# Sparse experts of a graph-network layer: row gathers four slots ahead, finished rows in buffers of their own, slot 0 always expert 0

## What is computed

```python
x = x + sparse(_layernorm(x))
# sparse:
gate_logits = x @ gate_w.T + gate_b + expert_bias        # 1250 x 8
top_idx = argmax(gate_logits, axis=-1)                   # one expert per row
for e in range(8):
    h = relu(x @ w1[e] + b1[e])                          # 1024 -> 512
    y = h @ w2[e] + b2[e]                                # 512 -> 1024
    out = out + (top_idx == e) * y
```

## Time and profile before

| what | us |
|---|---|
| median of 3 runs (2924.33 to 2933.4) | 2929.55 |
| the profiled execution | 2930.76 |
| its span | 2929.0 |
| TensorE busy | 2697.2 (92%) |
| VectorE busy | 1433.2 (49%) |
| ScalarE busy | 763.5 (26%) |
| GpSimd busy | 751.0 (26%) |

### The profile page before, as it was taken

One profiled execution on the slowest core, in us unless ns is written; L12 is line 12 of the kernel. 1 busy time (PEld: TensorE's weight loads), 2 busy tenths in 40 slices (PEclk: granted clock), 3 DMA queues, 4 the chain that ended last, 5 costly groups with the idle time before them and its releaser, 6 DMA issues.

```text
span 2929.0 us, 32304 instructions
## 1 busy us (share of the span) xinstructions
PE 2697.2 (92%) x11128; PEld 2018.5 (69%) x11128; DVE 1433.2 (49%) x2411; ACT 763.5 (26%) x1241; POOL 751.0 (26%) x738
## 2 busy tenths in 40 slices
PE   5998998889999979999999999999999997958887
PEld 3553333478888767888888888887777676836775
DVE  8886775555455481001001001007888887846543
ACT  2002221233233232112112112114444443114321
POOL 1326771000000004555400000104555450003333
PEclk9999999799999988999999999999999998978998
DMA  4016773023333231222222222226777784437763
GB/s 136 1 64 194 210 211 86 1 87 115 115 115 115 86 143 58 99 78 90 93 75 107 76 79 104 93 75 201 236 233 262 256 253 174 137 138 252 261 245 106
DMA packets 168160, 399.86 MB, mean 137 GB/s; under 512 B 25152, under 2 KB 25920, under 8 KB 168072
## 3 DMA queue, kind: packets, MB, share of 16 engines
q0 software_dynamic: 56384, 168.89, 18.7%
q1 hardware_dynamic: 84472, 180.00, 17.7%
q10 hardware_dynamic: 27216, 49.86, 4.6%
HBM read 327.74 MB, written 75.25 MB: 138 GB/s over the span
## 4 chain that ended last, share of the span: by engine, by line
PE 76%; DMA 9%; DVE 8%; issue 3%; ACT 2%; POOL 1%; DVEq 0%; ACTq 0%; POOLq 0%; SPq 0%
PE pair L899 10%; PE pair L901 10%; PE pair L900 10%; PE pair L795 5%; DMA out<-tok_x,tok_put 3%; DMA tok_x<-x_rows,tok_list 3%; PE pair L737 3%; PE pair L810 2%; PE pair L777 2%; PE pair L922 2%; PE pair L945 2%; PE pair L943 2%; PE pair L944 2%; PE pair L925 2%; PE pair L865 2%
## 5 line engine op out<-in xcount | busy, mean ns | idle before, releaser
L1560 DVE TENSOR_TENSOR wl<-raw,wh 128x512 fp32r<-128x512 f32 x328 | 205.4, 686 | 802.0 <-ACT wh L1062 801.9
L899 PE MATMUL pair<-wh,xh 128*128 128x512 f32 x1280 | 499.0, 390 | 1.7 <-DVE xl L1311 1.7
L901 PE MATMUL pair<-wl,xh 128*128 128x512 f32 x1280 | 498.7, 390 | 0.0
L900 PE MATMUL pair<-wh,xl 128*128 128x512 f32 x1280 | 498.6, 390 | 0.0
L658 POOL DMA_INDIRECT rows_y<-y_rows,l_row x184 | 222.3, 1208 | 303.6 <-PE pair L925 156.7
L1062 ACT ACTIVATE OS<-pair 128x512 f32<-128x512 f32 x170 | 101.5, 597 | 746.9 <-PE pair L901 693.4
L899 PEld LDWEIGHTS pair<-wh,xh 128*128 128x128 f32 x1280 | 240.8, 188 | 52.2 <-issue 2.1
L900 PEld LDWEIGHTS pair<-wh,xl 128*128 128x128 f32 x1280 | 240.8, 188 | 50.2
L901 PEld LDWEIGHTS pair<-wl,xh 128*128 128x128 f32 x1280 | 240.7, 188 | 50.0
L1062 ACT ACTIVATE high_y<-rows_y,l_inv 128x1024 fp32r<-128x1024 f32 x154 | 176.6, 1151 | 252.1 <-DMA rows_y<-y_rows,l_row 239.2
L1062 ACT ACTIVATE wh<-raw 128x512 fp32r<-128x512 f32 x328 | 194.0, 627 | 182.3 <-PE pair L867 140.5
(11 more groups left out here) (275 smaller groups left out, 4610.4 us busy)
## 6 DMA issues: line engine op xcount, KB each, us to landing
y_rows<-OS ACTq DMA_DIRECT2D x160, 256.0 KB, 2.0
raw<-in_L_gnn_weight SPq DMA_DIRECT2D x16, 2048.0 KB, 8.9
raw<-in_L_ffn_w SPq DMA_DIRECT2D x12, 2048.0 KB, 8.9
raw<-in_L_ffn_w SPq DMA_DIRECT2D x24, 1024.0 KB, 6.2
tok_raw<-in_L_ffn_w SPq DMA_DIRECT2D x7, 2048.0 KB, 10.9
tok_raw<-in_L_ffn_w SPq DMA_DIRECT2D x14, 1024.0 KB, 14.1
U<-in_L_ffn_b SPq DMA_DIRECT2D x18, 512.0 KB, 4.4
x_rows<-X SPq DMA_DIRECT2D x1, 5120.0 KB, 15.3
```

The lines of the kernel that those rows point to most:

```text
L899: mm(o, xh[:, k, cols], wh[:, k, :], start=(k == 0), stop=False)
L900: mm(o, xl[:, k, cols], wh[:, k, :], start=False, stop=False)
L901: last = mm(o, xh[:, k, cols], wl[:, k, :], start=False, stop=(k == KD - 1))
L1560: v.tensor_tensor(wl[:, k, :], raw[:, k, :], wh[:, k, :].bitcast(F32), ALU.subtract).then_inc(wl_ready, 1)
```

## The change

- Weights of expert 0 for slot 0 are loaded before the routing is known: w1, b1 and b2 as soon as the last rows of the stage before are mixed, w2 when the layer norm has read them and they are stored. ScalarE makes the high parts right behind the route matmuls, VectorE the low parts of w1 in two places of the routing (`first_w1_low`); the low parts of w2 stay where they were. `sort` gets `least=1`: expert 0 has at least one slot.
- The route matmuls of a group of rows stand between the transposes.
- The slot table is made by one wide compare, a reduce and a copy, the one-hot matrices by three wide operations, in fp32r.
- `tok_rows` has four buffers, and rows are gathered four slots ahead.
- `out_rows` writes into `tok_out`, two buffers of their own; GpSimd gathers the residual rows without a wait for the scatter, and waits for `out_done` behind its add, then raises `tok_out_free`, for which VectorE waits before it writes.
- TensorE's hardware loop over the slots is unrolled. The buffers of raw w2 change places.

```diff
-        tok_perm_lane = U[:, 2 * D:2 * D + NT * P].rearrange("p (t n) -> p t n", t=NT)
-        tok_perm_val = U[:, 4 * D:4 * D + NT * TSLOTS].rearrange("p (t s) -> p t s", t=NT)
-        tok_rows = U[:, 0:2 * D].rearrange("p (b n) -> p b n", b=2)
+        tok_perm_lane = place("tok_perm_lane", "u", [P, NT, P], F32R, skip=2 * D)
+        tok_perm_val = place("tok_perm_val", "u", [P, NT, TSLOTS], F32R, skip=4 * D)
+        tok_in_slot = U[:, 4 * D + HID:4 * D + HID + NT * TSLOTS].rearrange("p (t s) -> p t s", t=NT)
+        slot_past = U[:, 5 * D:5 * D + TSLOTS * (E1 - 1)].rearrange("p (s g) -> p s g", g=E1 - 1)
+        tok_rows = [place(f"tok_rows{i}", r, [P, D], skip=n) for i, (r, n) in enumerate((("u", 0), ("u", D), ("b2", 0), ("hot", 0)))]
...
-        tok_raw2 = [[place("tok_raw2_00", "xt", [P, KH, HALF], skip=16 * HALF), place("tok_raw2_01", "xn", [P, KH, HALF])],
-                    [place(f"tok_raw2_1{h}", "x", [P, KH, HALF], skip=(8 + 4 * h) * HALF) for h in range(2)]]
+        tok_raw2 = [[place(f"tok_raw2_0{h}", "x", [P, KH, HALF], skip=(8 + 4 * h) * HALF) for h in range(2)],
+                    [place("tok_raw2_10", "xt", [P, KH, HALF], skip=16 * HALF), place("tok_raw2_11", "xn", [P, KH, HALF])]]
+        tok_out = [place(f"tok_out{b}", "os", [P, D], skip=2 * b * HALF) for b in range(2)]
...
+            sp.wait_ge(mixed_ready, NT)
+            sp.dma_start(tok_raw1[0][:], a["L1_ffn_w1"][0].rearrange("(k p) n -> p k n", p=P)).then_inc(tok_w1_in[0], 16)
+            load_b1(0, 0)
+            load_b2(0, 0)
+            sp.wait_ge(xn_ready, 4 * NT)
+            sp.wait_ge(x4_stored, 16 * NT)
+            for h in range(2):
+                sp.dma_start(tok_raw2[0][h][:], a["L1_ffn_w2"][0, :, h * HALF:(h + 1) * HALF].rearrange("(k p) n -> p k n", p=P)).then_inc(tok_w2_in[0], 16)
             sp.wait_ge(xn_stored, 16 * NT)
-            sp.wait_ge(x4_stored, 16 * NT)
             sp.wait_ge(slot_exp_ready, 1)
-            for s in range(2):
-                e, new = slot_words(s)
-                load_w1(e, new, s)
-                load_b1(e, s)
-                load_w2(e, new, s)
-                load_b2(e, s)
+            e, new = slot_words(1)
+            load_w1(e, new, 1)
+            load_b1(e, 1)
+            load_w2(e, new, 1)
+            load_b2(e, 1)
...
-                pool.indirect_dma_start(out, bass.IndirectOffsetOnAxis(ap=tok_put[:, s:s + 1], axis=0), tok_x[s % 2][:], None,
+                pool.indirect_dma_start(out, bass.IndirectOffsetOnAxis(ap=tok_put[:, s:s + 1], axis=0), tok_out[s % 2][:], None,
...
-            for s in range(2):
-                gather(tok_rows[:, s, :], xn_dram, s, tok_rows_in[s])
+            for s in range(4):
+                gather(tok_rows[s][:], xn_dram, s, tok_rows_in[s])
+            pool.sem_inc(tok_out_free, 2)
             for s in range(TSLOTS):
-                if s + 2 < TSLOTS:
-                    pool.wait_ge(tx_full, 2 * s + 2)
-                    gather(tok_rows[:, s % 2, :], xn_dram, s + 2, tok_rows_in[s % 2])
                 if s >= 2:
                     scatter(s - 2)
-                    pool.wait_ge(out_done[s % 2], 16 * (s // 2))
                 gather(tok_x[s % 2][:], x3_dram, s, tok_x_in[s % 2])
+                if s + 4 < TSLOTS:
+                    pool.wait_ge(tx_full, 2 * s + 2)
+                    gather(tok_rows[s % 4][:], xn_dram, s + 4, tok_rows_in[s % 4])
                 pool.wait_ge(tok_b2_in[s % 2], 16 * (s // 2 + 1))
                 pool.wait_ge(tok_x_in[s % 2], 16 * (s // 2 + 1))
                 pool.tensor_tensor(tok_x[s % 2][:], tok_x[s % 2][:], tok_b2[:, s % 2, :], ALU.add).then_inc(tok_xb_ready, 1)
+                if s >= 2:
+                    pool.wait_ge(out_done[s % 2], 16 * (s // 2))
+                    pool.sem_inc(tok_out_free, 1)
...
-            transpose_x(T_LN4)
-            pe.wait_ge(t_read, T_LN4 + 2 * NT)
             pe.wait_ge(consts_in, 16 * 8)
-            route(V_ROUTE2, ((w_route2, XT),), E1, score_rows2)
+            for m in range(NT + 1):
+                if m < NT:
+                    pe.wait_ge(xn_ready, 3 * NT + m + 1)
+                    for j in range(2):
+                        transpose4(T_LN4 + 2 * m + j, [last_rows[m][:, (4 * j + q) * P:(4 * j + q + 1) * P] for q in range(4)])
+                for g, (lo, cnt) in enumerate(TOKG):
+                    if (lo + cnt) // P == m:
+                        pe.wait_ge(t_read, T_LN4 + 2 * m)
+                        pe.wait_ge(v_read, V_ROUTE2 + g - 1)
+                        for k in range(KD):
+                            last = mm(v_bank[(V_ROUTE2 + g) % 2][0:E1, 0:cnt], w_route2[:, k, :], XT[:, k, lo:lo + cnt],
+                                      start=(k == 0), stop=(k == KD - 1))
+                        last.then_inc(v_full, 1)
+            pe.wait_ge(v_read, V_ROUTE2 + len(TOKG))
...
-            transpose_rows(0, 0)
-            up(0, 0)
-            transpose_rows(1, 1)
-            transpose_h(0, first=True)
-            with pe.Fori(0, TSLOTS // 2 - 1) as i:
-                for b in (1, 0):
-                    s = 2 * i + (2 - b)
-                    up(s, b)
-                    transpose_rows(s + 1, 1 - b)
-                    transpose_h(s)
-                    down(s - 1, 1 - b)
-            last_s = TSLOTS - 1
-            up(last_s, 1)
-            transpose_h(last_s)
-            down(last_s - 1, 0)
-            down(last_s, 1)
+            transpose_rows(0)
+            for s in range(TSLOTS):
+                up(s, s % 2)
+                if s + 1 < TSLOTS:
+                    transpose_rows(s + 1)
+                transpose_h(s, first=(s == 0))
+                if s > 0:
+                    down(s - 1, (s - 1) % 2)
+            down(TSLOTS - 1, (TSLOTS - 1) % 2)
...
-            rows_high(0)
-            act.wait_ge(xn_stored, 16 * NT)
+            act.wait_ge(v_full, V_ROUTE2 + len(TOKG))
             act.wait_ge(tok_w1_in[0], 16)
             w1_high(0)
+            act.wait_ge(xn_stored, 16 * NT)
+            act.wait_ge(tok_w2_in[0], 32)
+            w2_high(0)
+            rows_high(0)
+            act.wait_ge(slot_exp_ready, 1)
             new, next_new = new_experts(0)
             rows_high(1)
             hidden_high(0, 0)
-            act.wait_ge(tok_w2_in[0], 32)
-            w2_high(0)
             act.wait_ge(tok_w1_in[1], 16)
             if_new(next_new, w1_high, 1, tok_w1h_ready)
...
+                if least:
+                    link(v.tensor_scalar(pre[:, 4, 0:least], pre[:, 4, 0:least], 1.0, None, ALU.max))
...
+            def first_w1_low(pieces):
+                for k in pieces:
+                    dve.wait_ge(tok_w1h_ready, k + 1)
+                    v.tensor_tensor(tok_w1l[:, k, :], tok_raw1[0][:, k, :], tok_w1h[:, k, :].bitcast(F32),
+                                    ALU.subtract).then_inc(tok_w1l_ready, 1)
+
+            v.sem_inc(tok_w1l_ready, 1)
...
-            sort(tok_key[:], E1, NT, tok_hot[:], tok_cum[:], tok_pos[:], v_bank[V_PRE2 % 2], V_PRE2, gsm[:, 0, :], gsm[:, 1, :])
-            slot_groups(slot_exp[:], slot_tmp[:], TSLOTS, E1)
+            sort(tok_key[:], E1, NT, tok_hot[:], tok_cum[:], tok_pos[:], v_bank[V_PRE2 % 2], V_PRE2, gsm[:, 0, :], gsm[:, 1, :],
+                 lambda: first_w1_low(range(0, 2)), least=1)
+            link(v.tensor_tensor(slot_past, iota_free[:, 0:TSLOTS].unsqueeze(2).broadcast_to([P, TSLOTS, E1 - 1]),
+                                 pre[:, 5, 0:E1 - 1].unsqueeze(1).broadcast_to([P, TSLOTS, E1 - 1]), ALU.is_ge))
+            link(v.tensor_reduce(slot_tmp[:], slot_past, AX.X, ALU.add))
+            link(v.tensor_copy(slot_exp[:], slot_tmp[:]))
...
-            for t in range(NT):
-                v.tensor_scalar(tok_perm_lane[:, t, :], iota_free[:, 0:P], tok_lane[:, t:t + 1], None, ALU.is_equal)
-                last = v.tensor_scalar(tok_perm_val[:, t, :], iota_free[:, 0:TSLOTS], tok_slot[:, t:t + 1], tok_id[:, t:t + 1],
-                                       ALU.is_equal, ALU.mult)
-            last.then_inc(tok_perm_ready, 1)
+            v.tensor_tensor(tok_in_slot, iota_free[:, 0:TSLOTS].unsqueeze(1).broadcast_to([P, NT, TSLOTS]),
+                            tok_slot[:].unsqueeze(2).broadcast_to([P, NT, TSLOTS]), ALU.is_equal)
+            link(v.tensor_tensor(tok_perm_lane[:], iota_free[:, 0:P].unsqueeze(1).broadcast_to([P, NT, P]),
+                                 tok_lane[:].unsqueeze(2).broadcast_to([P, NT, P]), ALU.is_equal))
+            v.tensor_tensor(tok_perm_val[:], tok_in_slot, tok_id[:].unsqueeze(2).broadcast_to([P, NT, TSLOTS]),
+                            ALU.mult).then_inc(tok_perm_ready, 1)
+            first_w1_low(range(2, KD))
...
+                dve.wait_ge(tok_out_free, s + 1)
                 for h in range(2):
                     cols = slice(h * HALF, (h + 1) * HALF)
                     dve.wait_ge(down_full, 2 * s + (h + 1))
```

(4 more changed lines are left out.)

14 lines of the change are left out of this document (8 added, 6 removed).

## The result

| what | before | after |
|---|---|---|
| median, us | 2929.55 | 2909.41 (5 runs, 2901.47 to 2913.2) |
| ratio, 95% interval | | 0.9931 (0.9911 to 0.995) |
| the profiled execution, us | 2930.76 | 2910.61 |
| its span, us | 2929.0 | 2908.8 |

A forecast was written before the change was run, and what follows sets the result against it. The prediction saw the last stretch bound by GpSimd's chain of scatter, gather and add, with 36.6 us of loop stalls. Entry 5.2, loop 19.1 and end 2.5 sum to 26.8 us saved: forecast 2903 us, range 2888 to 2919.

The forecast's parts named there:

- The entry: From routing to slot 1: token list 4.1 us earlier, first gather 0.5, slot 0's matmuls 0.6; 5.2 us saved.
- The first gather: Gather of slot 0's rows: 8.0 us from issue to use instead of 8.45, 0.5 saved.
- The pause ahead of slot 1: TensorE's 6.94 us idle before slot 1's matmuls stays, set by VectorE splitting slot 0's w2 first.
- The end: After the last matmul: no wait for GpSimd's add and only the second half left, 2.5 us saved.
- The mechanism of the loop: Slot loop: own buffers and earlier gathers remove row and scatter waits; VectorE becomes late where neighbouring slots are both new.
- The loop's size: Slots 1 to 17: stalls of 17.5 us instead of 36.6, 19.1 saved.
- the price of a pair: Two neighbouring slots with new weights: 4.5 us stall, between 1.5 and 6.75; three pairs, 13.5.
- one hit: Of four w2 runs at lone new slots, one meets GpSimd's add and stalls the loop: 4 us, between 0 and 16.
- The rival in which every add wins the port: Loop: pairs cost 5.75 us each, all four lone w2 runs are hit at 3.9; 2918 us, chance 0.15.
- if more than three slots stall (then it is the port): Loop: sign that the forecast is wrong, the cause being the port shared by VectorE and GpSimd.
- SP's earlier start: Loop weight loads: w1 starts some 20 us ahead of use, against 10.9 us to land.
- The eighth expert: Empty expert 0 gets a slot: 4 MB more and a third pair of neighbouring new slots.

The follow-up runs named there:

- e6: Changed kernel with VectorE's low parts of slot 0's w2 made while it waits for the first gather; median 2944.39 us, ratio 0.991.
- e5: Changed kernel with SP loading w1 of slot s + 1 ahead of b1, w2 and b2 of slot s; median 2947.03 us, ratio 0.9911.
- e4: Changed kernel without GpSimd's add of b2, so its output has no b2; median 2905.07 us, ratio 0.9922.
- e2: Changed kernel with the loop part undone, keeping the new entry and expert 0's own slot; median 2937.11 us, ratio 1.0029 to before.
- e11: As e2, with experts 0 and 1 exchanged in the tables so that seven experts are loaded; median 2924.16 us, ratio 0.9994 to before.
- e3: Changed kernel with experts 0 and 1 exchanged in the tables so that seven experts are loaded; median 2910.08 us, ratio 0.9937 to before.
- e1: Kernel before with the loop part alone: four row buffers, own buffers for finished rows, TensorE's loop unrolled; median 2911.39 us, ratio 0.9941.
- e12: The repeat: the changed kernel run once more, unchanged; median 2910.19 us, ratio 0.9945 to before.
- e10: As e9, with b2 added to the residual rows by VectorE and not by GpSimd; median 2896.91 us, ratio 0.9892 to before.
- e9: Changed kernel with the edits of e5 and e6 together; median 2896.70 us, ratio 0.9903 to before.

## Why the prediction was right, and where it was off

By the two spans the change saves 20.2 us where the sum had 26.8. Of the 6.6 missing, 4.4 are in the loop and 2.7 ahead of M; entry and end came out 0.5 better.

*The entry held in the sum, 5.2 forecast and 5.3 found.* By steps: the list matmuls start when VectorE's wide operations are done, 7.99 us of idle against 11.36, and the list stands 5.0 us earlier (4.1 forecast). The list matmuls take 2.30 for 4.46, but VectorE reads the result (at 2628.34) only behind its six w1 pieces, as costed:

```profile
2624.73 3.69 DVE L1794 TENSOR_TENSOR tok_w1l<-tok_raw,tok_w1h 128x512 fp32r<-128x512 f32 x6
```

The first gather gave 0.1 (0.5 forecast; it takes 8.3 us, as in the crowded row of before), slot 0's matmuls 0.7 (0.6). The pause ahead of slot 1 was forecast unchanged and grew from 6.94 to 9.17, because GpSimd's add now began inside the w2 run of slot 0 (7.04 us in after, 4.90 in before). The matmuls from there to slot 1's h-transpose took 8.05 us instead of 9.33, which gives 1.3 of it back. So the sum of the entry agrees in part by luck: 0.9 more at the list and 1.3 at these matmuls made up for the 2.2 us by which the pause grew. Reading VectorE's order, and not the name in the wait, was right (e6).

*The end held*, 2.9 for 2.5: last matmul 2899.49, last scatter 2901.44.

*The mechanism of the loop held.* The row waits and the scatter wait went, and what ends TensorE's waits is VectorE's bias add. The sign of the forecast and three quarters of its size come from that.

*The loop's size was off*: 19.1 forecast, 14.7 found and 12.6 in the repeat. The stalls beyond 12.37 a slot were to be 17.5 us and are 21.9. The h-transposes come late by 1.3 us at slot 2, 7.0 at 9 and 5.5 at 15 (13.8), and by 1.6 at slot 3, 2.0 at 5, 2.8 at 10 and 1.7 at 16 (8.1). The forecast had 13.5 for the pairs and 4 for the w2 runs behind them, but that 13.8 is so near to 13.5 is luck. The loss of clock behind a pause was part of its price of a pair, and it shows at the slot after. The h-transposes of slots 15 and 16:

```profile
2860.98 1.12 PE L1048 MATMUL pair<-ident,U 128*128 128x128 f32 x4 [5.35 <-DVE U L1867]
...
2875.09 0.66 PE L1048 MATMUL pair<-ident,U 128*128 128x128 f32 x4
```

They lie 14.11 us apart, 1.7 more than a slot, though TensorE has no idle time between them and the w2 run of slot 15 takes 4.90: the down matmuls behind the pause of 5.35 take 0.63 us each until 2864.0, and 0.39 from 2864.4 on (granted clock 0.88 from 2861.5 to 2873.5). At slot 10, 1.1 of the 2.8 us are idle time and 1.7 such loss. Counted this way the pairs cost 1.3, 8.7 and 7.2, together 17.2 us where the sum had 13.5, and the hits at slots 3, 5 and 10 1.6 + 2.0 + 1.1 = 4.7 where it had 4. So two steps failed. The first is the price of a pair, 4.5 us with at most 1 of it for late w1. ScalarE waited for w1 at slots 9 and 15, 6.4 us in two places (see the waits after), and with w1 in time (e5) the stalls there are 1.3 and 3.3. The second is "one hit" of 4 us: there were three, each of half that price or less, so the sum of this term came out near by luck. I had placed GpSimd's adds at 8.5 to 11 us of a slot, away from w2 runs. The timelines of VectorE and of GpSimd from slot 2 to slot 4 show what happens instead:

```profile
2675.84 4.89 DVE L1883 TENSOR_TENSOR tok_w2l<-tok_raw,tok_w2h 128x512 fp32r<-128x512 f32 x8
...
2688.39 6.33 DVE L1883 TENSOR_TENSOR tok_w2l<-tok_raw,tok_w2h 128x512 fp32r<-128x512 f32 x8
...
2697.30 7.12 DVE L1877 TENSOR_TENSOR tok_w1l<-tok_raw,tok_w1h 128x512 fp32r<-128x512 f32 x8
2704.34 1.27 DVE L1899 TENSOR_TENSOR tok_out<-pair,tok_x 128x512 f32<-128x512 f32 x2
...
2714.72 6.72 DVE L1883 TENSOR_TENSOR tok_w2l<-tok_raw,tok_w2h 128x512 fp32r<-128x512 f32 x8
```

```profile
2676.78 4.84 POOL L683 DMA_INDIRECT out<-tok_out,tok_put  x1 [19.02 <-DVE tok_out L1899]
...
2687.54 2.41 POOL L698 TENSOR_TENSOR tok_x<-tok_x,U 128x1024 f32<-128x1024 f32 x1 [3.41 <-DMA tok_x<-x_rows,tok_list]
...
2697.39 2.85 POOL L698 TENSOR_TENSOR tok_x<-tok_x,U 128x1024 f32<-128x1024 f32 x1 [2.47 <-DMA tok_x<-x_rows,tok_list]
...
2706.45 1.00 POOL L683 DMA_INDIRECT out<-tok_out,tok_put  x1 [6.20 <-DVE tok_out L1899]
...
2714.22 2.41 POOL L698 TENSOR_TENSOR tok_x<-tok_x,U 128x1024 f32<-128x1024 f32 x1 [4.27 <-DMA tok_x<-x_rows,tok_list]
```

The scatter at 2676.78, which I had costed at 1.0 us of issue, takes 4.84 and ends 0.9 us behind the w2 run at 2675.84. The gather behind it and the add start that much later, and the add (2687.54) reaches the next w2 run (2688.39, 6.33 us). The add at 2697.39 stretches the w1 run to 7.12 us. `out_rows` is queued behind that run, so finished rows come late, and with them the scatter (2706.45), the gather behind it and the add (2714.22), which now meets the next w2 run (2714.72, 6.72 us). A collision or a long issue pushes the next add into the next run; that is read from the order of these rows, and no run takes one collision away alone. The count of stretched runs is hardly higher (7 of 15, and 5 of 14 before), but 5 of the 8 w2 runs are among them, and 1 of 7 before: the adds moved from the w1 runs, where there was slack, to the w2 runs, behind which the next slot's bias add stands. The rival in which every add wins the port (the third case of the range) had the mechanism, though not the count or the price of a hit; e4 shows what all adds together cost in the loop, 7.0 us (9.1 against the repeat).

The prediction's own sign, "if more than three slots stall (then it is the port)", came true: seven stall by more than 1 us. But the cause it names is only part of it. Without any add five still do (e4: slots 2, 9, 10, 15, 16), with late w1 and the loss of clock behind it.

e5 puts late w1 at 5 to 7 us for the loop. So SP's earlier start, for which I had given w1 20 us of room, was true only for lone slots; for a pair, the wait for w2's split (51.1 to 91.8 us) took the place of that for the add.

*The eighth expert* I had noted as a burden. e2 against e11 puts it at 18.1 us of loop in the old chain, 9.4 by the medians; in the new one e3 shows none. The gain of the loop part is therefore larger than the difference of the two kernels tells: 28.4 us with expert 0's slot in both (e2 to after; 28 by the medians), of which 13.7 only make good what e2's loop loses against before.

*The 2.7 us ahead of M* were in no step. The stage before the last layer norm, where GpSimd gathers rows, has the same code in both; first and last matmul of its line, before and after:

```profile
L943 PE MATMUL pair<-wh,xh x320: 387/389/793, 1983.5 to 2414.7; 128*128 128x512 f32 x160
```

```profile
L956 PE MATMUL pair<-wh,xh x320: 387/389/1219, 1983.1 to 2418.7; 128*128 128x512 f32 x160
```

It lasts 431.2 us before and 435.6 after. In the traces of e1 to e12 it lasts 434.5 to 441.3, so before's is the shortest of all fourteen, and that would also fit medians that save less than the sums. But of before there is one trace only; whether its stage is truly shorter, and by what, stays open. The 1.6 us by which e10's last stretch is shorter than e9's are within this noise; their medians are equal.

The Trainium skill's rule ("SBUF — State Buffer", section "SBUF: two separate sides"), that VectorE and GpSimd exclude each other at their shared port for a whole instruction, agrees with e4 and e10, where no run of eight exceeds 5.02 us without GpSimd's adds, and with the add at 2714.22, which began ahead of its run. The add of 6.99 us in before still speaks against it to the letter.

## What to carry to other kernels

When a chain that crosses engines is cut, look at what becomes late next on the engine that is now the releaser, and follow its queue through one stretched instruction: what is queued behind it decides where the next collision falls. Read the order of the waiting engine before believing a wait's name; two moves of a few lines (w2's split into the first gather's wait, w1's load ahead of the neighbour's w2) gave 15 us of the last stretch here (13.5 by the medians), where the whole change gave 21 to 23 (15.5 to 20.1 by the medians). A burden such as an empty expert showed a price here only while the chain had no slack: measure it in the kernel in which it will run.

## What was not expected of the hardware

- A GpSimd add that starts shortly before a run of VectorE's two-input operations costs it only what is left of it: the add of 2.41 us at 2687.54 and the run at 2688.39 that took 6.33 for 4.9, 1.4 us more.
- An indirect DMA took GpSimd 0.93 to 1.5 us to issue in the slots of after, but two scatters took 4.84 us at 2676.78 and 4.86 at 2773.93. Both began within 1 us behind the start of a w2 run of VectorE (2675.84 and 2773.02, 4.89 us each) and ended 0.9 us behind its end. Others that began inside such a run took 1.3 to 1.5 us, so what makes the difference stays open.
- The list matmuls in fp32r take 2.30 us in 10 records against 4.46 in 20: half the records, half the time, at 18 columns each.
- The span of one unchanged stage with gathers varies by up to 10 us between the fourteen traces (431.2 to 441.3), more than several steps of this study.
